# Feed-forward layers: moments taken a round ahead, norm and low-rank product at other steps, four products instead of six, first chunk turned while the weights come

## What is computed

```python
def _L0_ffn_ref(x, fast_b, w_fc, w_proj, u, v, gate):
    def _bitlinear(x, w_latent):
        scale = jnp.clip(jnp.mean(jnp.abs(w_latent), axis=1, keepdims=True), 1e-05, None)
        tern = jnp.clip(jnp.round(w_latent / scale), -1.0, 1.0)
        return x @ (tern * scale).T
    h = _bitlinear(x, w_fc) + gate * (x @ v.T @ fast_b.T @ u.T)
    r = jnp.maximum(h, 0.0)
    return _bitlinear(r * r, w_proj)
x = x + _L0_attn_a_ref(_layernorm(x), ...)
x = x + _L0_ffn_ref(_layernorm(x), ...)
x = x + _L0_attn_b_ref(_layernorm(x), ...)
x = x + _L0_ffn_ref(_layernorm(x), ...)
```

## Time and profile before

| | |
|---|---|
| median of 3 runs | 3644.09 us (3638.44 to 3647.27) |
| the profiled execution, its own time | 3638.03 us |
| its span, first to last instruction | 3636.2 us |
| ffn1, from the first weight load to the last scaling | about 869 to 1276 us of the span |
| ffn2, from the first load to the last scaling | about 3249 to 3631 us |
| busy share of TensorE, VectorE, ScalarE, GpSimd | 91%, 69%, 55%, 21% |
| mean granted TensorE clock | 0.933 of full speed |

### The profile page before, as it was taken

The page is one execution under the profiler, slowest core; times in us unless marked ns, Lnnn a source line. Parts: engine busy times, 40 slices in busy tenths (PEclk is TensorE's granted clock), DMA queues, the critical chain, the costliest instruction groups (busy, mean ns, idle before and its releaser), DMA issues. The chain is left out here.

```text
span 3636.2 us, 78012 instructions
## 1 busy us (share of the span) xinstructions
PE 3315.7 (91%) x31460; PEld 1957.4 (54%) x31460; DVE 2503.2 (69%) x4755; ACT 2009.9 (55%) x2991; POOL 758.0 (21%) x887
## 2 busy tenths in 40 slices
PE   7999999995899939999999999999999999968998
PEld 4556555554677714444444444444444444427777
DVE  6676667663677717777767778687786776807776
ACT  3444444441555503666666667666676666755554
POOL 3444444342121110102011020110110201011112
PEclk8888888885999966999999999999999999989999
DMA  1000000001111142122222212122121312120110
GB/s 49 14 25 25 13 25 25 19 13 60 61 47 47 36 93 39 25 43 50 38 37 51 42 46 43 28 59 42 46 42 23 65 33 44 22 74 30 49 51 30
DMA packets 110471, 145.76 MB, mean 40 GB/s; under 512 B 21632, under 2 KB 94352, under 8 KB 109328
## 3 DMA queue, kind: packets, MB, share of 16 engines
q1 hardware_dynamic: 109344, 137.95, 16.1%
q0 software_dynamic: 768, 2.82, 0.4%
HBM read 53.99 MB, written 38.41 MB: 25 GB/s over the span
## 5 line engine op out<-in xcount | busy, mean ns | idle before, releaser
L1767 DVE TENSOR_REDUCE b_half_max<-banks 128x1 f32<-128x512 f32 x2048 | 1314.4, 685 | 443.2 <-PE banks L1492 261.6
L1718 ACT ACTIVATE b_p_t<-banks 128x1024 f32<-128x1024 f32 x1024 | 1047.0, 1025 | 397.3 <-PE banks L1492 256.0
L1548 PE MATMUL banks<-b_k_stack,b_q_stack 62*128 62x512 f32 x2048 | 828.9, 477 | 34.2 <-issue 17.8
L1609 PE MATMUL banks<-b_q_stack,b_k_stack 64*128 64x512 f32 x2048 | 851.7, 469 | 0.0
L1564 PE MATMUL banks<-b_p_t,b_v 128*17 128x256 f32 x8192 | 640.9, 385 | 25.1 <-ACT b_pv L1687 24.5
L1609 PEld LDWEIGHTS banks<-b_q_stack,b_k_stack 64*128 64x128 f32 x2048 | 342.9, 185 | 432.2 <-issue 416.7
L1492 PE MATMUL banks<-b_tables,b_halves 64*128 64x128 bf16 x4096 | 437.0, 224 | 0.0
L1548 PEld LDWEIGHTS banks<-b_k_stack,b_q_stack 62*128 62x128 f32 x2048 | 337.5, 188 | 68.6 <-issue 25.4
L1108 ACT ACTIVATE ffn_relu<-banks,ffn_scale_fc 128x512 f32<-128x512 f32 x256 | 176.3, 689 | 274.2 <-PE banks L1044 274.2
L1057 PE MATMUL banks<-ffn_proj_t,ffn_r_hi 128*128 128x256 f32 x1024 | 257.0, 285 | 2.5 <-DVE ffn_r_lo L1227 2.5
L1564 PEld LDWEIGHTS banks<-b_p_t,b_v 128*17 128x17 f32 x8192 | 135.9, 95 | 225.3 <-issue 76.6
(11 more groups left out here) (231 smaller groups left out, 4948.1 us busy)
## 6 DMA issues: line engine op xcount, KB each, us to landing
ffn_x<-x SPq DMA_DIRECT2D x32, 512.0 KB, 3.9
b_q_stack<-b_qk_hi SPq DMA_DIRECT2D x256, 64.0 KB
b_k_stack<-b_qk_hi SPq DMA_DIRECT2D x256, 64.0 KB
a_x<-hidden_states SPq DMA_DIRECT2D x16, 512.0 KB, 3.9
x<-a_x SPq DMA_DIRECT2D x16, 512.0 KB, 2.9
x<-ffn_x SPq DMA_DIRECT2D x16, 512.0 KB, 2.9
b_x<-x SPq DMA_DIRECT2D x8, 1024.0 KB, 5.6
b_k_stack<-b_qk_lo SPq DMA_DIRECT2D x128, 64.0 KB
```

Source lines behind the costliest of these rows:

```text
L1548: last = pe.matmul(m, q_stack[rows, slot, qb * P:(qb + 1) * P], k_stack[rows, slot, half * BANK:(half + 1) * BANK], start=True, stop=not h ...
L1609: last = pe.matmul(out, k_stack[stack, slot, kb * P:(kb + 1) * P], q_stack[stack, slot, half * BANK:(half + 1) * BANK], start=True, stop=n ...
L1718: act.activation(p_t[use % P_BUFS][:, :, :], scores[use % 2], ACT.Exp, scale=slopes()[pair][0]).then_inc(p_made, 1)
L1767: dve.tensor_reduce(half_max[:, (pair + rg * PAIRS) * QB + qb, half:half + 1], misc.at["max", g, turn], axis=AX.X, op=ALU.max, negate=True ...
```

## The change

In the steady rounds:

- `normalize` has 8 steps instead of 7. The moments and 1/sqrt of chunk c + 1 are taken at the last step of `normalize(c)`, so a round before they were. The transposes stand at steps 2 and 3 instead of 3 and 4, and VectorE's `xn` stays at step 1.
- The low-rank product has four products instead of six. Its weights are laid out in 80 rows instead of 96, so that the product of the weights' rest comes out in rows of its own.
- The product stands at step 5 instead of behind the last one, with ScalarE's and VectorE's part of it, and `up` waits for `low` in front of the first product that reads it, behind four others.

At the start of each call:

- Chunk 0 is loaded first, and is normed, turned and cut while the weights come or, in ffn1, before they are prepared. `prepare_weights`, or in ffn2 the wait for the kept tiles, stands inside `normalize(0)`, in front of the low-rank product.
- In the preparation VectorE finds both scales first, so that GpSimd's comparison of the second matrix no longer waits for VectorE's work between. The low-rank weights `u` are cut on VectorE before they are turned, and ScalarE copies the turned ones.
- `ident` is loaded from the constants in both calls and is no longer kept.

The sizes and TensorE's part of the diff:

```diff
-        COPIES = 3
-        ROWS = COPIES * SUB
+        MAIN_ROWS, HI_ROWS, LO_ROWS = (0, 2 * RANK, 4 * RANK), (0, RANK, 2 * RANK), 4 * RANK
+        ROWS = 5 * RANK
...
-        NORMALIZE, UP, DOWN = 7, HT, 2 * CT
+        NORMALIZE, UP, DOWN = 8, HT, 2 * CT
...
             def normalize(c):
                 x_hi, x_lo = x_hi_bufs[c % 2], x_lo_bufs[c % 2]
-                yield
-                yield
-                yield
+                yield from steps(2)
...
-                yield
+                if c == 0:
+                    prepare_weights()
                 yield
                 b = normal[(3 * c + 2) % 2]
                 pe.wait_ge(x_lo_made, 2 * c + 2)
-                passes = [(kt, w, s) for kt in range(KT) for w, s in ((low_hi, x_hi), (low_hi, x_lo), (low_lo, x_hi))]
+                passes = [(kt, w, s) for kt in range(KT) for w, s in ((low_by_hi, x_hi), (low_by_lo, x_lo))]
...
                 last.then_inc(low_ready, 1)
+                yield from steps(3)
...
-                pe.wait_ge(low_made, c + 1)
...
+                    if m == 0:
+                        pe.wait_ge(low_made, c + 1)
                     pe.matmul(b, u3_t[:, cols], low[:, :], start=False, stop=True).then_inc(h_ready, 1)
```

VectorE's part, with the preparation's new order and `normalize` (`take_moments` is the old first part of it, made a function):

```diff
+                find_scales(fc, HT, KT, scale_fc, 0, 0)
+                dve.wait_ge(weights_in, 16 * WEIGHTS)
+                find_scales(proj, KT, HT, scale_proj, HT, 3)
+                dve.reciprocal(gate_fc[:, :], scale_fc[:, :]).then_inc(u_steps, 1)
                 make_ternary(fc, HT, KT, 0, turned)
...
+                dve.tensor_copy(u_hi[:, :, :], u[:, :, :]).then_inc(u_steps, 1)
+                dve.wait_ge(u_steps, 4)
...
+            def normalize(c):
+                x, x_hi, x_lo, low = xs[c % X_BUFS], x_hi_bufs[c % 2], x_lo_bufs[c % 2], low_bufs[c % 2]
+                if c == 0:
+                    take_moments(c)
                 yield
...
                 yield
-                yield
                 for kt in range(KT):
...
-                yield
+                if c == 0:
+                    prepare_weights()
                 yield
                 dve.wait_ge(low_hi_made, c + 1)
                 dve.tensor_tensor(low[SUB:2 * SUB, :], normal[(3 * c + 2) % 2][SUB:2 * SUB, :],
                                   low[SUB:2 * SUB, :].bitcast(F32), ALU.subtract).then_inc(low_made, 1)
+                yield from steps(2)
+                if c + 1 < CHUNKS:
+                    take_moments(c + 1)
+                yield
```

ScalarE's copy of the turned `u`, and the loads:

```diff
+                    if out_t is proj_t:
+                        for m in range(HT):
+                            act.wait_ge(u_turned, m + 1)
+                            act.activation(u3_t[:, m * P:(m + 1) * P], banks[0:ROWS, 5 + m % 2, 0:P], ACT.Copy).then_inc(u_t_made, 1)
...
+            load(0)
+            sp.dma_start(ident[:, :], d["c_ident"]).then_inc(ident_in, 16)
             if first_use:
-                sp.dma_start(fc[:, :, :], d["w_fc"].rearrange("(m p) n -> p m n", p=P)).then_inc(first_in, 16)
-                sp.dma_start(ident[:, :], d["c_ident"]).then_inc(first_in, 16)
+                sp.dma_start(fc[:, :, :], d["w_fc"].rearrange("(m p) n -> p m n", p=P)).then_inc(fc_in, 16)
```

More of the change, by code:

```diff
@@ L969, in prepare_weights @@
             def prepare_weights():
+                if not first_use:
+                    pe.wait_ge(kept_moved, 16 * len(kept))
+                    return
                 def turn_ternary(turns, first_row):
@@ L1063, in down @@
                     yield
-            if first_use:
-                prepare_weights()
-            else:
-                pe.wait_ge(kept_moved, 16 * len(kept))
+            pe.wait_ge(ident_in, 16)
             schedule(down, up, normalize)
@@ L1117, in down @@
                     yield
-            if first_use:
-                prepare_weights()
-            else:
-                act.wait_ge(kept_moved, 16 * len(kept))
             schedule(down, up, normalize)
@@ L1126, in prepare_weights, with find_scales @@
             def prepare_weights():
-                def find_scales(w, rows, cols, scale, base):
+                if not first_use:
+                    dve.wait_ge(kept_moved, 16 * len(kept))
+                    return
+                def find_scales(w, rows, cols, scale, first_row, base):
+                    these = slice(first_row, first_row + rows)
                     dve.tensor_reduce(scale[:, 0:rows], w[:, :, :], axis=AX.X, op=ALU.add,
@@ L1239, in down @@
                     yield
-            if first_use:
-                prepare_weights()
-            else:
-                dve.wait_ge(kept_moved, 16 * len(kept))
             schedule(down, up, normalize)
@@ L1268, in normalize @@
                 pool.tensor_tensor(norm_rstd[:, :], norm_rstd[:, :], minus_half[:, :], ALU.pow).then_inc(norm_scale, 1)
-                for _ in range(NORMALIZE):
-                    yield
+            def normalize(c):
+                if c == 0:
+                    take_rstd(c)
+                yield from steps(4)
+                if c == 0 and first_use:
+                    prepare_weights()
+                yield from steps(3)
+                if c + 1 < CHUNKS:
+                    take_rstd(c + 1)
+                yield
             def up(c):
@@ L1311, in sync @@
                 sp.dma_start(gate[:, :], d["gate"].to_broadcast([P, 1])).then_inc(weights_in, 16)
-                for c in range(X_BUFS - 1):
+                for c in range(1, X_BUFS - 1):
                     load(c)
@@ L1321, in sync @@
             else:
-                load(0)
                 for name, t in kept.items():
```

86 lines of the change are left out of this document (41 added, 45 removed).

## The result

The changed kernel takes **3586.2 us** (median of 4 runs, 3581.61 to 3589.31); the kernel before, on the same chip, 3641.27 us (4 runs, 3636.02 to 3647.27). The ratio is 0.9845, with a 95% interval of 0.9831 to 0.9859: 55 us less, where 63 were summed. 3586.2 lies in the range, 7 us above the forecast.

What follows compares the result with a forecast made beforehand. TensorE's queue was taken to set the pace, with waits for `low` and `xn` each round. Rounds (2 x 18.2), run-ins (2 x 3.3) and starts (10.2 + 10) sum to 63 us less, from 3642 to 3579 us; range 3562 to 3605.

Steps and rivals of the forecast that it cites:

- `low`, -1.28: In a steady round, TensorE's wait for `low` before `up` goes, as its reader stands further behind: -1.28 us.
- `xn`, +0.3: In a steady round, the wait for `xn` before the transposes stays, since VectorE's second cut is late: +0.3 us.
- `r_lo`, +0.15: In a steady round, a new wait for the last cut before the eighth row pair of `down`: +0.15 us.
- The round, -1.3: Sum of the steady round's terms: -1.3 us a round, 14 rounds in each call.
- Run-in, -3.3: The run-in round of each call loses products and the `low` wait, and gets `xn` earlier: -3.3 us a call.
- Start of ffn2, -10.2: At ffn2's start, chunk 0's work is hidden under the weights' load and the `low` wait is covered: -10.2 us.
- Start of ffn1, -10: At ffn1's start, preparation begins later but ends where it did, with chunk 0 already done: -10 us.
- Rival A: VectorE's chain sets the round; the wait for `xn` takes up what `low` gives back: 3606 us, chance 0.13.
- B: VectorE comes level in the rounds and the wait for `xn` falls to about 1 us: 3551 us, chance 0.08.
- C: Moments at the round's end delay the cuts and the wait for `xn` grows: slower, 3681 us, chance 0.02.
- D: The starts hide nothing because chunk 0 lands late, and A as well: about 15 us less or none, chance 0.02.
- E: In ffn1's preparation, VectorE's small copies wait until both GpSimd comparisons are over, about 3 us later: 3582 us, chance 0.25.

Runs made afterwards that it cites:

- six_products: The changed kernel with the two products of low_by_lo and x_lo made twice, so the low-rank product is six products again; 3598.01 us.
- narrow_addition: The changed kernel with GpSimd's residual addition covering only 8 of 256 columns; 3559.41 us.
- start_undone: The changed kernel with ffn1's weight preparation and ffn2's wait for the kept tiles back at the head of every engine's program; 3597.95 us.
- comparison_held: The changed kernel with GpSimd's two comparisons of the second matrix held until VectorE has made its small copies of `u`; 3586.24 us.
- turn_later: The changed kernel with the transposes, and what hangs on them, one step later in `normalize`; 3521.99 us.
- moments_late: The changed kernel with moments and 1/sqrt back in the round of their own chunk, the transposes still at step 2; 3650.71 us.

## Why the prediction was right, step by step

The mechanism held but for one term, the new wait for `r_lo`, which was put too low by 0.33 us a round, 9 us in all. The calls gave 58.8 us of the 63 all the same, since `xn` lost 2 us less than forecast and the starts gave 2.5 us more. That these made up for over half of it is luck. The medians differ by 55 us and the calls by 58.8; the other 4 us lie within the mixer's scatter from one execution to the next.

- **Four products, -0.47.** Right; six_products gives 0.44 back.
- **`low`, -1.28.** Right as read in the rows: no wait is left. But the term was not the move's alone. With the product back at its old place behind the new transposes the kernel loses 0.84 us there, and none for `r_lo`.
- **`xn`, +0.3.** Measured +0.22 (1.88). The cause was right: the second cut is what is late, `xn` follows it at once and meets the addition. Of the 1.88 us, 0.42 are the addition's and go with it (narrow_addition).
- **`r_lo`, +0.15, between 0 and 0.4.** This is the step that failed: 0.48. The prediction had the cut ready 2.74 to 3.1 us behind TensorE and counted the delay before the eighth pair alone. It was 3.15 us behind in the rows (in a second round TensorE goes on at 3408.32 and the cut ends at 3411.47), since its CAST meets the addition of the fourth scaling. The addition was named as a risk for the second cut, not for the last, and narrow_addition shows what it costs: without it 0.09 of the 0.48 us are left.
- **The round, -1.3.** Measured -1.07 (21.06, just above the 20.7 to 20.9 stated): -0.47 - 1.28 + 0.22 + 0.48 = -1.05. Over 28 rounds the 0.23 us less are 6.4 us.
- **Run-in, -3.3.** Measured -3.7 in ffn2. In ffn1 it gave about 0.9 us less than in ffn2 (from the fifth product of `up(0)` to that of `up(1)` 19.85 before and 16.95 after, against 19.87 and 16.03); the granted clock from 921.4 to 930.0 us was 0.82, that of ffn2's run-in 0.98.
- **Start of ffn2, -10.2.** Measured -11.8: -2.62 behind the low-rank product, as forecast (-2.6), and -9.15 ahead of it, where 7.57 were forecast. The tiles landed 13.2 us after the first issue instead of 14.8. Start_undone and six_products, with the same loads, have 14.2 and 14.5 us, comparison_held and turn_later 13.0 and 13.6. So the landing scatters by about as much as it gained, and how much of the 1.6 us the smaller tiles give isn't shown.
- **Start of ffn1, -10.** Measured -10.9. The preparation ended where it was forecast (39.6 us after the issue, stated 38 to 42), and chunk 0 was done. It began 5.0 us later, as forecast, but not for the reason given: by start_undone, 2.8 us of that come from weights that are there later, behind chunk 0's load, and 2.2 from VectorE's work on it. The rest is TensorE's clock, which was at the 2.4 GHz level for the products behind it: 2.6 us, not 3.4.
- **Rival A** (the waits move, 3606) is refuted: the round is under 21.6. **B** (level, 3551) is refuted for the change, but turn_later shows where its gain lay: one step more between VectorE and its reader. **C** (slower) is refuted, though moments_late shows that such a kernel exists, and that it is worse than its waits by the clock. **D** is refuted.
- **E** (the copies wait for both comparisons, +3 us). Half right. The CAST of `u` began at 903.99 and ended at 905.02; the first comparison ends at 902.10 + 2.83 = 904.93. That is a wait for the end of GpSimd's instruction, as the low-rank CASTs of comparison_held waited until 907.16. The Trainium skill (SBUF — State Buffer, section Who interferes with whom) says of the shared port pair that whichever of the two comes second is blocked for the whole instruction of the other, and the trace agrees in these two places. But the three copies behind it were over at 906.37, while the second comparison ran until 907.76. So only one comparison was waited out; the preparation lost 1.4 us by it and not 3. What let the copies through isn't settled.

## What to carry to other kernels

When an in-order engine is kept waiting, look at the distance between the row that makes the operand and the row that asks for it before shortening either: one step of distance gave 64 us here and took no work away, while the whole change gave 55. Add the losses from start to start over a round, with the wait-free round as the check; a waits' view can show a loss of 0.2 us a round only at the weight loads, where it is easily passed over. And where two engines' elementwise work meets, price the meeting at every place where a moved instruction can land, not only at the first.

## What the runs showed of the hardware

- In moments_late TensorE stood still for 2.27 us once a round. In twelve of ffn2's 14 rounds its granted clock fell to the 1.2 GHz level behind that for some 3 us, and 1.54 us were lost; in two, behind the same wait, it stayed at 1.00. With a wait shorter by 1 us (the changed kernel) it was 1.00 over all 14 rounds.
- VectorE's CAST of 128x512 took 0.84 us beside a GpSimd addition and 0.43 alone, the four parts of `xn` 1.78 and 1.38, and the addition itself 1.24 and 0.74. The addition took 0.74 beside the CAST as well, which began after it; it took 1.24 where it began 0.03 us behind `r_lo`'s subtraction (0.69 us), and in that place even the one cut to 8 columns took 0.73 us, where it took 0.20 elsewhere. So whichever began second was drawn out. A small CAST that met a GpSimd comparison took 1.03 us and 0.23 alone; a copy of 16 columns out of PSUM beside the same comparison took 0.17 us as always.
- The mixer, with the same instructions, took 868.9 to 879.1 us in twelve profiled executions, and the kept tiles landed 13.0 to 14.5 us after the first issue with the same loads.
